# Edge-row products of the destination stage on two partition ranges, relu by halves, and the turn of x2 ahead of the second layer

## The reference, cut to what matters

```
feat = concat([x, out1, out2, out3, u[batch]], axis=1)   # 128 + 48 + 48 + 48 + 16
h    = relu(feat @ W1 + b1)                               # 256 wide
x    = layernorm(x + (h @ W2 + b2 + x))
```

## Time and profile before

| | |
|---|---|
| time, median of 3 runs | 6279.33 us (6278.2 to 6283.3) |
| the profiled execution, its own time | 6277.28 us |
| its span, first to last instruction | 6275.5 us |
| busy share of the span | PE 72%, DVE 70%, POOL 69%, PEld 51%, ACT 50% |
| DMA | 1090.56 MB, mean 174 GB/s |
| granted TensorE clock, mean | 0.875 |

### The profile page before, as it was taken

The page is one execution under the profiler, slowest core; times in us unless marked ns, Lnnn a source line. Parts: engine busy times, 40 slices in busy tenths (PEclk is TensorE's granted clock), DMA queues, the critical chain, the costliest instruction groups (busy, mean ns, idle before and its releaser), DMA issues. The chain is left out here.

```text
span 6275.5 us, 102230 instructions
## 1 busy us (share of the span) xinstructions
PE 4503.8 (72%) x25328; PEld 3191.3 (51%) x25328; DVE 4371.1 (70%) x8168; ACT 3114.7 (50%) x6471; POOL 4344.4 (69%) x4339
## 2 busy tenths in 40 slices
PE   1079899997886999999889999978887884432200
PEld 0057688886665777777744444444444442211100
DVE  8966799987886888888733334369999995753300
ACT  0057688885664555555533333348888883110000
POOL 0056677777777777777766666657777776777777
PEclk9999999999999999999999999988888885555555
DMA  1033588887897999999755555534444446953311
GB/s 30 7 87 109 169 250 248 252 239 226 283 287 218 257 262 263 263 262 263 212 163 164 167 165 163 164 113 115 113 115 115 115 116 204 328 171 96 96 42 40
DMA packets 896637, 1090.56 MB, mean 174 GB/s; under 512 B 137109, under 2 KB 543521, under 8 KB 895492
## 3 DMA queue, kind: packets, MB, share of 16 engines
q1 hardware_dynamic: 757158, 816.08, 43.4%
q0 software_dynamic: 137984, 221.55, 13.8%
q10 hardware_dynamic: 1344, 51.38, 2.1%
HBM read 652.84 MB, written 497.99 MB: 183 GB/s over the span
## 5 line engine op out<-in xcount | busy, mean ns | idle before, releaser
L970 PE MATMUL bank<-ident,gat 128*128 128x128 f32 x2352 | 430.5, 312 | 627.7 <-DVE zT L1945 551.5
L1080 PE MATMUL bank<-W2s,hT 128*128 128x128 f32 x6272 | 777.1, 277 | 77.6 <-ACT hT L1336 77.6
L1065 PE MATMUL bank<-x1T,W1x 128*128 128x512 f32 x1568 | 773.1, 605 | 30.5 <-ACT x1T L1255 26.9
L1080 PEld LDWEIGHTS bank<-W2s,hT 128*128 128x128 f32 x6272 | 733.9, 192 | 103.6 <-ACT hT L1336 102.2
L970 PEld LDWEIGHTS bank<-ident,gat 128*128 128x128 f32 x2352 | 298.3, 161 | 776.2 <-issue 582.5
L1265 ACT ACTIVATE mbuf<-t 128x512 f32<-128x512 f32 x490 | 310.1, 633 | 711.2 <-DVE t L1979 440.8
L1336 ACT ACTIVATE hT<-bank,b1u 128x512 f32<-128x512 f32 x784 | 491.4, 677 | 245.2 <-PE bank L1068 236.3
L1924 DVE TENSOR_TENSOR gat<-gat,pays 128x512 f32<-128x512 f32 x392 | 270.6, 690 | 425.5 <-DMA gat<-X,pays 366.5
L970 PE MATMUL bank<-ident,x 128*128 128x128 f32 x3136 | 487.1, 278 | 107.6 <-DVE x L1912 84.9
L722 POOL DMA_INDIRECT gat<-X,d_x x392 | 392.8, 1002 | 222.2 <-issue 222.2
L735 POOL DMA_INDIRECT Y<-x,d_out x392 | 405.0, 1033 | 176.4 <-issue 116.4
(11 more groups left out here) (366 smaller groups left out, 11529.4 us busy)
## 6 DMA issues: line engine op xcount, KB each, us to landing
X<-x SPq DMA_DIRECT2D x588, 256.0 KB, 3.0
fB<-row_s_same SPq DMA_DIRECT2D x392, 256.0 KB
Y<-x SPq DMA_DIRECT2D x294, 256.0 KB, 3.8
xT<-in_x_fm SPq DMA_DIRECT2D x196, 256.0 KB
ffB<-rows_last_notlast SPq DMA_DIRECT2D x98, 512.0 KB
out_rows<-Y ACTq DMA_DIRECT2D x28, 1792.0 KB, 10.4
Z1T<-zT SPq DMA_DIRECT2D x98, 256.0 KB
Z1E<-zE SPq DMA_DIRECT2D x98, 256.0 KB
```

The lines of the kernel that those rows point to most:

```text
L970: mm = pe.transpose(dst[:, t, :], tiles[t], ident[:, :])
L1065: mm = pe.matmul(bH[h][:, :, :], W1x[:, cols], x1T[s][:, :], start=True, stop=kind != "d")
L1080: mm = pe.matmul(bMLP[:, t, :], hT[h][s][:, t * P:(t + 1) * P], W2s[:, h, :], start=False, stop=h == HC - 1, skip_group_check=True)
```

## The change

The matrix W1m (the 48 rows of W1 for the mean) is loaded twice, into partitions 0 to 47 and 64 to 111, and so is each group's `mnt`. `chain_b2` starts with the two products over the mean, half 0 on partitions 0 to 47 into bH0 and half 1 on partitions 64 to 111 into bH1, and then does, for each half, the product of `att` and that of x1T. After half 0 it raises a new semaphore `half_hidden`. `relu` waits for `half_hidden` ahead of its first half and for `hidden` ahead of its second. On PE `chain_d1` stands ahead of `chain_c`; on DVE `x2_carry` stands ahead of `layer2`.

```diff
@@ constants (SP)
-                         (W1m[0:AF, :], W1[P + 2 * AF:P + 3 * AF, :])):
+                         (W1m[0:AF, :], W1[P + 2 * AF:P + 3 * AF, :]),
+                         (W1m[AM:AK, :], W1[P + 2 * AF:P + 3 * AF, :])):
@@ att_load (SP)
-                sp.dma_start(mnt[s][0:AF, :], MNT[:, epos(g)]).then_inc(S("ld_att", s), 16)
+                for first in (0, AM):
+                    sp.dma_start(mnt[s][first:first + AF, :], MNT[:, epos(g)]).then_inc(S("ld_att", s), 16)
@@ chain_b2 (PE)
                 if kind == "d":
-                    ready(pe, "ld_att", s, i, 32)
+                    ready(pe, "ld_att", s, i, 48)
+                    for h in range(HC):
+                        rows = slice(h * AM, h * AM + AF)
+                        pe.matmul(bH[h][:, :, :], W1m[rows, h * P:(h + 1) * P], mnt[s][rows, :], start=True,
+                                  stop=False)
                 for h in range(HC):
                     cols = slice(h * P, (h + 1) * P)
-                    mm = pe.matmul(bH[h][:, :, :], W1x[:, cols], x1T[s][:, :], start=True, stop=kind != "d")
                     if kind == "d":
                         pe.matmul(bH[h][:, :, :], W1a[0:AK, cols], att[s][0:AK, :], start=False, stop=False)
-                        mm = pe.matmul(bH[h][:, :, :], W1m[0:AF, cols], mnt[s][0:AF, :], start=False, stop=True)
+                    mm = pe.matmul(bH[h][:, :, :], W1x[:, cols], x1T[s][:, :], start=kind != "d", stop=True)
+                    if kind == "d" and h == 0:
+                        mm.then_inc(S("half_hidden", s), 1)
@@ the loop (PE)
-            steps(pe, EI, (of("d", chain_b1), 0), (of("d", chain_c), 2), (of("d", chain_d1), 3),
+            steps(pe, EI, (of("d", chain_b1), 0), (of("d", chain_d1), 3), (of("d", chain_c), 2),
                   (of("d", chain_b2), 1), peeled=1)
@@ relu (ACT)
-                    ready(act, "hidden", s, c)
+                    if kind != "d":
+                        ready(act, "hidden", s, c)
                     for h in range(HC):
+                        if kind == "d":
+                            ready(act, ["half_hidden", "hidden"][h], s, [i, c][h])
                         a = act.activation(hT[h][s][:, :], flat(bH[h]), ACT.Relu, bias=b1u[:, h:h + 1])
@@ the loop (DVE)
-            steps(dve, EI, (x2_select, 3), (layer2("d"), 2), (x2_carry, 3), (power("d", 1), 2), (norm2("d"), 2), peeled=1)
+            steps(dve, EI, (x2_select, 3), (x2_carry, 3), (layer2("d"), 2), (power("d", 1), 2), (norm2("d"), 2), peeled=1)
```

More of the change, by code:

```diff
@@ L630, in att_load @@
             def att_load(i, s):
-                if void(sp, i, s, ("ld_att", i, 32), ("ld_last", i, 16)):
+                if void(sp, i, s, ("ld_att", i, 48), ("ld_last", i, 16)):
                     return
@@ L912, in _ @@
                                   skip_group_check=True)
-                        pe.wait_ge(S("ld_const"), 16 * 19)
+                        pe.wait_ge(S("ld_const"), 16 * 20)
                         for c in range(HC):
@@ L1056, in chain_b2 @@
                 c = ci(kind, i)
-                if kind != "node" and void(pe, i, s, ("hidden", c, 1)):
+                if kind == "s" and void(pe, i, s, ("hidden", c, 1)):
+                    return
+                if kind == "d" and void(pe, i, s, ("half_hidden", i, 1), ("hidden", c, 1)):
                     return
@@ L1536, in flags_beside @@
                 elif n == 6:
-                    dve.wait_ge(S("ld_const"), 16 * 19)
+                    dve.wait_ge(S("ld_const"), 16 * 20)
                     dve.wait_ge(S("ident"), 1)
```

## The result

The median is 6183.9 us (6179.89 to 6187.76, 4 runs) against 6281.32 (6278.2 to 6285.68, 4 runs) of the kernel before: a ratio of 0.9841, 95% interval 0.9829 to 0.9854, 1.6% faster. The forecast was 6153 us, range 6142 to 6193. So the change was faster, and POOL took over the bound from PE, as forecast; but of a forecast gain of 128 us only 97 came. The question is where the other 31 us are.

A forecast was written before the change was run, and what follows sets the result against it. PE was taken to bound the stage (busy 889 of 995 us), with POOL next. At POOL's pace, -118.7 up to group 97's gather and -7.4 in the tail, together -126, took 6277.28 to 6151.3; plus 2.05: 6153 us, range 6142 to 6193.

The forecast's parts named there:

- the pair: PE's two products over the mean: half a product, 0.43 us, free by overlap; bounds none and 1.05; together 1.67.
- Relu's wait: PE's wait of 0.94 us a step ahead of the second layer: two turns, 0.98, cover the remaining 0.90.
- the 8.3 of the prediction: PE's step in us after the change, with half a product side by side; 8.76 if apart, 7.7 with all.
- x2_carry ahead of layer2: DVE's order: the scan is done 2.6 us after the turn's start, the second layer 2.60, so t2 loses nothing.
- the margins: x2 done at S + 7.0 at most, S being the step's start, wanted at S + 9.2: margin 2.2 us.
- SP's further load: One more load a group, 0.44 us of issue, hidden by SP's 5.1 us wait; if not hidden, 42 us.
- wait of the turn for x2: Sign of the slower rival: on PE, x2's turn ahead of the second layer becomes the wait; 6326 us, chance 0.03.
- The landing of the gathers: No-change rival: gathered rows turned 15.2 us after the gather's start keep the step at 9.96; 6279 us, chance 0.04.
- POOL's own pace: POOL's gathers (5.06) and scatters (1.307 each) in the stage, without waiting for PE: 8.69 us a group.
- 0.17 of the first gather after a wait: 0.17 us a group taken off POOL's grouped rows of 9.98, with 1.12 of idle, to reach 8.69.
- its own case, POOL's pace: POOL sets the stage's pace at 8.69 us a group: 6153 us, own range 6145 to 6163, chance 0.74.
- the rival in which PE stays the bound: Mean products do not overlap, or relu's second half is uncovered: PE's step 8.76 or 9.02, 6164 or 6189 us; chance 0.17.

The follow-up runs named there:

- the parts alone: The kernel before with one part each: the two orders 6240.96 us, relu by halves 6223.78 us, the two mean products first on two ranges 6184.73 us.
- one_range: The changed kernel with both products over the mean on partitions 0 to 47, mnt and W1m loaded once: 6198.72 us.
- second_scan: The changed kernel with one more DVE scan of two SBUF operands in each step, after norm2: 6245.04 us.
- both_psum: The changed kernel with x2_select's product in idle bank bSK and this stage's t2 in idle bank bT1: 6150.93 us.

## Why the prediction was right, and where it was off

**The bound was found.** PE bounds the stage before, and POOL, which followed through t2, is the next: no wait of POOL for PE is left, and the pair, the one part that alone brings PE under POOL's pace, is enough. By their ratios the parts alone bring 46 (orders), 62 (halves) and 99 us (pair), all three together 100. What the first two bring shows only as long as PE is the bound.

**Relu's wait and the order.** The second half was covered as reckoned (0.98 of turns over 0.90). The orders alone were put at 48 us and measured 46, the halves at 60 and measured 62.

**The pair.** Half a product was taken as free, bounds none and one; one is free (1.06). The page "TensorEngine Tiling (Array Packing)" of the Trainium skill, section "Tiling Modes", had it: different tiles can run in parallel. The trace agrees (1.06 for both on two ranges, 1.91 on one). My own reading, that the two records of one product must follow those of the other, fell. The sum goes by POOL's pace, so in it the size of this term makes no difference; no run has PE at the 8.3 of the prediction, but one_range, at 8.4, is 15 us slower, and its gathers are the longer ones.

**x2_carry ahead of layer2 and the margins.** x2 is in time, SP's further load is hidden, and no wait of the turn for x2 appears. The landing of the gathers never held POOL.

**The term that was mis-sized.** "POOL's own pace is 5.06 + 2.776 x 1.307 = 8.69" measured 9.03, 33.6 us over 97 groups. The 5.06 came from the first groups, when DVE ran no scan; and of the grouped rows I took off "0.17 of the first gather after a wait", which was the scan's hold, met by one gather in four in the scan's last 0.4 us. Once POOL goes at its own pace, it meets the scan at any place. With both DVE instructions reading at most one operand from SBUF, the pace is 8.694 and the time 6150.93.

**The range.** The prediction gave its own case, POOL's pace, 6145 to 6163, and the measured 6183.9 lies outside. It lies inside 6142 to 6193 only because that range also took in the rival in which PE stays the bound (6164 to 6189), and that is not what happened. That the range held is luck; that the bound went from PE to POOL is not, since the waits show it.

The page "SBUF — State Buffer" of the Trainium skill, section "Who interferes with whom", states that a DVE instruction with two SBUF inputs contends with a GpSimd instruction that reads SBUF, and one with at most one input there does not, outside the two-port modes. All of these runs agree (gathers that start in the scan take 1.320 us with two operands in SBUF, 0.981 with one). The prediction did not weigh that rule; it would have been a rival of its own, with its price in the rows' 1.16.

## What to carry to other kernels

When a change hands the bound to another engine, measure that engine's pace while its neighbours run as they will after the change, not in a stretch where they are idle. A duration that is always a little longer at one place is a question: here 0.17 us off the path was the first sign of 33 us on it. And where GpSimd issues indirect DMAs back to back and sets the pace, a DVE operand moved from SBUF to an idle PSUM bank can bring what a further gain on PE cannot: here 33 us, with PE's free step of 7.66 already under POOL's.

## What the runs showed of the hardware that was not expected

An indirect DMA's instruction on GpSimd that starts inside a DVE scan of two SBUF operands, from 0.11 us after the scan's start to 0.2 us before its end, ends 0.75 to 0.83 us after that scan, gathers and scatters alike (the changed kernel, one_range, second_scan). One that started ahead of the scan, or at most 0.06 us into it, is not held: none of these took over 1.02 us in the changed kernel. Two float32 products of 48 rows, on partitions from 0 and from 64 and into two banks, took 1.06 us together, against 1.91 on the same range. And PE's mean granted clock in the stage was 0.95 in the changed kernel, with falls to the lower level (1.2 GHz) beside single waits of 2.2 to 3.3 us for a gather; from 3200 to 3950 it was 0.96 there, and 1.00 in both_psum, where PE waits about as long in all (79.0 us against 81.3) but at most 2.2 us at once. POOL, which bounds the stage, had no pause over its issue gap in either.
